# Adapter products of two tiles in one slot, one job four steps later, and the half job's second product in f16

## The reference, cut to what matters

```python
# x: (16 batches, 128 tokens, 128 features)
def moe(x, gates, shared_prob):                    # 8 experts and a shared one, F = 512
    g, u = einsum('bsd,edf->ebsf', x, Wg), einsum('bsd,edf->ebsf', x, Wu)
    experts = einsum('be,ebsd->bsd', gates, einsum('ebsf,efd->ebsd', silu(g) * u, Wd))
    shared = (silu(x @ Sg) * (x @ Su)) @ Sd
    return (1 - shared_prob) * experts + shared_prob * shared

def adapter(x, language):                          # A = 32, one of 10 languages per batch
    h = relu(einsum('bsh,bha->bsa', x, W1[language]) + b1[language])
    y = x + einsum('bsa,bah->bsh', h, W2[language]) + b2[language]
    return layernorm(y) * gamma[language] + beta[language]

x = x + moe(x, ...)
x = x + adapter(x, language)
```

## Time and profile before

| what | value |
| --- | --- |
| time, median of three runs | 297.66 us |
| time of the profiled execution | 297.04 us |
| its span | 295.2 us |
| PE busy | 290.1 us, 98% |
| DVE busy | 268.8 us, 91% |
| ACT busy | 231.1 us, 78% |
| POOL busy | 19.3 us, 7% |
| PE in the chain that ended last | 94% |

### The profile page before, as it was taken

The page is one execution under the profiler, slowest core; times in us unless marked ns, Lnnn a source line. Parts: engine busy times, 40 slices in busy tenths (PEclk is TensorE's granted clock), DMA queues, the critical chain, the costliest instruction groups (busy, mean ns, idle before and its releaser), DMA issues.

```text
span 295.2 us, 5086 instructions
## 1 busy us (share of the span) xinstructions
PE 290.1 (98%) x1510; PEld 144.3 (49%) x1510; DVE 268.8 (91%) x585; ACT 231.1 (78%) x517; POOL 19.3 (7%) x32
## 2 busy tenths in 40 slices
PE   8999999999999999999999999999999999999995
PEld 2444444444444444444444444444444444588883
DVE  5999999998989898988989999999999999977795
ACT  6998878788878787877897788887878876667771
POOL 3200201100000000000002010001100011000011
PEclk9999999999999999999999999999999999999999
DMA  6973110244000000000011001010001110000001
GB/s 208 385 307 109 52 65 19 62 120 112 2 2 0 0 2 0 0 2 1 1 22 26 18 9 39 12 25 19 17 3 39 27 18 10 2 36 3 0 2 36
DMA packets 17940, 13.39 MB, mean 45 GB/s; under 512 B 11486, under 2 KB 15994, under 8 KB 17914
## 3 DMA queue, kind: packets, MB, share of 16 engines
q1 hardware_dynamic: 17482, 12.86, 14.4%
q10 hardware_dynamic: 432, 0.21, 0.2%
HBM read 11.23 MB, written 1.05 MB: 42 GB/s over the span
## 4 chain that ended last, share of the span: by engine, by line
PE 94%; DVE 2%; DMA 1%; SPq 1%; issue 1%; ACT 0%; POOL 0%; POOLq 0%; DVEq 0%
PE moe_ps L449 10%; PE moe_ps L446 10%; PE moe_ps L447 10%; PE gate_ps L400 10%; PE up_ps L426 10%; PE up_ps L431 10%; PE up_ps L423 10%; PE gate_ps L403 10%; PE gate_ps L408 10%; DMA w_full<-weights 1%; DVE hidden L680 1%; PE adapt_ps L458 0%; DVE gx_lo L649 0%; SPq L319 0%; DVE h_lo L686 0%
## 5 line engine op out<-in xcount | busy, mean ns | idle before, releaser
L563 ACT ACTIVATE silu<-gate_ps 128x512 f32<-128x512 f32 (+1 forms) x160 | 88.2, 551 | 45.3 <-PE gate_ps L408 44.3
L680 DVE SCALAR_TENSOR_TENSOR hidden<-silu,up_ps 128x512 f32<-128x512 f32 (+1 forms) x160 | 100.3, 627 | 19.2 <-PE up_ps L431 11.6
L686 DVE TENSOR_TENSOR h_lo<-hidden,h_hi 128x512 f16<-128x512 f32 (+1 forms) x160 | 102.4, 640 | 0.2
L568 ACT ACTIVATE h_hi<-hidden 128x512 f16<-128x512 f32 (+1 forms) x160 | 92.8, 580 | 9.2 <-DVE hidden L680 8.4
L426 PE MATMUL up_ps<-gx_lo,w_hi 128*128 128x512 f16 (+1 forms) x160 | 57.3, 358 | 0.4 <-DVE gx_lo L649 0.4
L400 PE MATMUL gate_ps<-x_hi,w_hi 128*128 128x512 f16 (+1 forms) x160 | 57.4, 359 | 0.0
L431 PE MATMUL up_ps<-gx_hi,w_lo 128*128 128x512 f16 (+1 forms) x160 | 57.3, 358 | 0.0
L423 PE MATMUL up_ps<-gx_hi,w_hi 128*128 128x512 f16 (+1 forms) x160 | 57.3, 358 | 0.0
L403 PE MATMUL gate_ps<-x_lo,w_hi 128*128 128x512 f16 (+1 forms) x160 | 57.3, 358 | 0.0
L446 PE MATMUL moe_ps<-h_hi,w_hi 128*128 128x512 f16 (+1 forms) x160 | 57.3, 358 | 0.0
L449 PE MATMUL moe_ps<-h_lo,w_hi 128*128 128x512 f16 (+1 forms) x160 | 57.3, 358 | 0.0
(11 more groups left out here) (88 smaller groups left out, 148.6 us busy)
## 6 DMA issues: line engine op xcount, KB each, us to landing
w_full<-weights SPq DMA_DIRECT2D x8, 768.0 KB, 9.2
affine_sb<-affine SPq DMA_DIRECT2D x16, 128.0 KB, 2.9
x_full<-xT SPq DMA_DIRECT2D x3, 256.0 KB, 8.6
x<-x_blocks SPq DMA_DIRECT2D x48, 16.0 KB, 1.8
out_dram<-result SPq DMA_DIRECT2D x3, 256.0 KB, 2.1
w_full<-weights SPq DMA_DIRECT2D x4, 128.0 KB, 3.0
w_full<-w2b SPq DMA_DIRECT2D x24, 16.0 KB
w_full<-weights SPq DMA_DIRECT2D x1, 256.0 KB, 3.8
```

The lines of the kernel that those rows point to most:

```text
L563: nc.scalar.activation(silu_slot(n), gate_ps[n % 2][:, 0:STEPS[n][4]], ACT.Silu, scale=1.0 / W_SCALE).then_inc(silu_ready, 1)
L568: nc.scalar.activation(h_slot(h_hi, n), hidden_slot(n), ACT.Copy).then_inc(h_hi_ready, 1)
L680: nc.vector.scalar_tensor_tensor(out=hidden_slot(n), in0=silu_slot(n), scalar=HIDDEN_RESCALE, in1=up_ps[n % 2][:, 0:STEPS[n][4]], op0=ALU. ...
L686: nc.vector.tensor_tensor(h_slot(h_lo, n), hidden_slot(n), h_slot(h_hi, n), ALU.subtract).then_inc(h_lo_ready, 1)
```

## The change

Three things change. The job of tile 0 starts at step 75 instead of 71 and that of tile 1 at 95 instead of 91; `moe_out` stays where a tile's sum is ready (`moe_at`: steps 71 and 75), for which `x2T`, `w1_sb` and `b1_sb` get a second place. `adapter_in` of tiles 0 and 1 is issued together, in step 76 (`in_step`), into the two halves of each 256 columns of `adapt_ps`; tile 1's `w1` and `b1` are loaded at the start. Job 3 makes its second product as the others do: f16 parts on 98 rows, with `w2_upper` at at-8 (step 139), `w2_lower` at at-6, `h_upper` at at+4, `h_others` at at+4, two f16 matmuls at at+7 and one 256-wide `y`.

```diff
-JOBS = [(0, 0, BATCHES, down_step(0, 0) + 1), (1, 0, BATCHES, down_step(0, 0) + 21),
+JOBS = [(0, 0, BATCHES, down_step(1, 0) + 1), (1, 0, BATCHES, down_step(1, 0) + 21),
         (2, 0, BATCHES, down_step(2, 0) + 1), (TILES - 1, 0, BATCHES // 2, down_step(TILES - 1, 0) + 1)]
+def moe_at(j):
+    return down_step(JOBS[j][0], 0) + 1
+def in_step(j):
+    return JOBS[0 if j == 1 else j][3] + in_at(j)
 def back_at(j):
-    return 6
+    return 6 if j < MOVED else 7
+def w2_at(j):
+    return 0 if j < MOVED else -8
-        w1_sb = sb("w1_sb", [P, BATCHES * A], F32)
+        w1_sb = sb("w1_sb", [P, 2 * BATCHES * A], F32)
-        x2T = sb("x2T", [P, N], F32)
+        x2T = sb("x2T", [P, 2 * N], F32)
...
-            load_adapter(0)
+            load_adapter(0, True, True)
+            load_adapter(1, True, False)
...
-                    load_adapter(t + 1)
+                    load_adapter(t + 1, t > 0, True)
...
-                pe.wait_ge(adapter_loaded, adapter_count(t))
-                if j > 0:
+                pe.wait_ge(adapter_loaded, adapter_count(0 if t == 1 else t))
+                if j > 1:
                     pe.wait_ge(y_ready, BEFORE[j])
                 for q in range(first, first + count):
-                    last = nc.tensor.matmul(fourth(adapt_ps, q)[:, 0:S], cols(w1_sb, q, A), cols(x2T, q, S),
+                    last = nc.tensor.matmul(cols(fourth(adapt_ps, q), place(t), S, A), w1_of(t, q), cols(x2T_of(t), q, S),
                                             start=True, stop=True, tile_position=(0, q * A))
...
-                pe.wait_ge(adapt_h_ready, count)
-                pe.wait_ge(x2_ready, 1)
+                pe.wait_ge(w2_lower_ready, j + 1)
+                pe.wait_ge(h_others_ready, 2 * (j + 1))
+                if j >= MOVED:
+                    pe.wait_ge(x2_ready, 1)
                 for q in range(first, first + count):
-                    last = nc.tensor.matmul(cols(back_ps[q % 2], q // 2, D), stacked(adapt_h, q, S, A + 1),
-                                            stacked(w2b2_sb, q, D, A + 1), start=True, stop=True)
+                    last = nc.tensor.matmul(cols(x2_ps, q, D), cols(h_stack, q, S, STACK), cols(w2_stack, q, D, STACK),
+                                            start=True, stop=True)
...
-                if since == 2 and j < MOVED:
+                if since == w2_at(j) + 2:
                     w2_lower(j)
-                if since == 4 and j < MOVED:
+                if since == (in_at(j) + 3 if j < MOVED else in_at(j) + 2):
                     h_others(j)
```

More of the change, by code:

```diff
@@ L200, in build @@
         x2_ps = bank("x2_ps")
-        back_ps = [adapt_ps, x2_ps]
         last_tile = TILES - 1
@@ L276, in adapter_count, with place, w1_of, b1_of @@
         def adapter_count(t):
-            return 16 * BATCHES * (6 * (t + 1) if t < last_tile else 6 * t + 3)
+            return 16 * (8 * BATCHES, 12 * BATCHES, 18 * BATCHES, 18 * BATCHES + 6 * (BATCHES - TAIL[2]) + 3 * TAIL[2])[t]
+        def place(t):
+            return 1 if t == 1 else 0
+        def w1_of(t, q):
+            return cols(w1_sb, place(t) * BATCHES + q, A)
+        def b1_of(t, q):
+            return fourth(b1_sb, q)[:, place(t):place(t) + 1]
+        def x2T_of(t):
+            return cols(x2T, place(t), N)
         def fourth(tensor, q):
@@ L337, in _, with load_adapter @@
             sp.wait_ge(ids_loaded, 16)
-            def load_adapter(t):
+            def load_adapter(t, first, second):
                 for q in range(BATCHES):
@@ L342, in load_adapter @@
                     one = bass.ds(lang, 1)
-                    sp.dma_start(cols(w1_sb, q, A), w1[one].rearrange("l h a -> (l h) a")).then_inc(adapter_loaded, 16)
+                    if first:
+                        sp.dma_start(w1_of(t, q), w1[one].rearrange("l h a -> (l h) a")).then_inc(adapter_loaded, 16)
+                        sp.dma_start(b1_of(t, q), b1[one].rearrange("l a o -> (l a) o")).then_inc(adapter_loaded, 16)
                     w2b2_q = w2b2[one].rearrange("l a h -> (l a) h")
-                    if t == last_tile:
+                    if second and t == last_tile and q >= TAIL[1]:
                         sp.dma_start(stacked(w2b2_sb, q, D, A + 1), w2b2_q).then_inc(adapter_loaded, 16)
-                    else:
+                    elif second:
                         w2_q = cols(w2_full, q, D, STACK)
@@ L519, in _ @@
                 if i == 0:
-                    pe.wait_ge(adapt_h_ready, JOBS[-1][2] + 1)
+                    pe.wait_ge(adapt_h_ready, 1)
                 else:
@@ L585, in w2_upper @@
                     act.wait_ge(back_done, j)
-                nc.scalar.activation(w2_stack[:, :], w2_full[:, :], ACT.Copy, scale=W_SCALE).then_inc(w2_upper_ready, 1)
+                width = JOBS[j][2] * D
+                nc.scalar.activation(w2_stack[:, 0:width], w2_full[:, 0:width], ACT.Copy,
+                                     scale=W_SCALE).then_inc(w2_upper_ready, 1)
             def h_upper(j):
                 act.wait_ge(h_full_ready, BEFORE[j + 1])
-                nc.scalar.activation(h_stack[0:A, :], h_full[:, :], ACT.Copy, scale=H_SCALE).then_inc(h_upper_ready, 1)
+                width = JOBS[j][2] * S
+                nc.scalar.activation(h_stack[0:A, 0:width], h_full[:, 0:width], ACT.Copy,
+                                     scale=H_SCALE).then_inc(h_upper_ready, 1)
             def copy_x2(j):
@@ L626, in _ @@
                 for j, (_, _, _, at) in enumerate(JOBS):
-                    if n == at and j < MOVED:
+                    if n == at + w2_at(j):
                         w2_upper(j)
@@ L630, in _ @@
                         adapter_relu(j)
-                    if n == at + in_at(j) + 2 and j < MOVED:
+                    if n == at + in_at(j) + 2:
                         h_upper(j)
@@ L723, in norm_stats @@
                         dve.wait_ge(x2_ready, 1)
[L724 to L729 removed]
+                    width = JOBS[j][2] * D
+                    nc.vector.scalar_tensor_tensor(out=y[:, 0:width], in0=x2_ps[:, 0:width], scalar=OUT_RESCALE,
+                                                   in1=x2[:, 0:width], op0=ALU.mult,
+                                                   op1=ALU.add).then_inc(y_ready, JOBS[j][2])
                 if i == 0:
@@ L787, in _ @@
                 hidden_of(n)
-                for j, (_, _, _, at) in enumerate(JOBS):
-                    if n == at:
+                for j in range(len(JOBS)):
+                    if n == moe_at(j):
                         moe_out(j)
```

47 lines of the change are left out of this document (16 added, 31 removed).

## The result

The changed kernel takes 300.19 us (median of six runs, 299.3 to 300.55), the kernel before 297.61 us in the same comparison (297.28 to 298.52). The ratio is 1.008, with a 95% interval of 1.0065 to 1.0095: by the ratio the change costs 2.4 us, by the two medians 2.6. The prediction said 298.4 us, in 297.2 to 299.0. Its sign was right, its size of 0.7 us about a third of what was measured, and the time lies outside its range. The profiled execution took 299.3 us, with a span of 297.5 us at a granted clock of 0.998.

What follows compares the result with a forecast made beforehand. PE, busy for 98% of the span, was taken as the bound. A net +0.52 us from the moved jobs and +0.18 us from the half job gave +0.70 us on 297.66, so 298.4 us, range 297.2 to 299.0.

Steps and rivals of the forecast that it cites:

- Its sign: Whole kernel: the change makes it slower, by a sum of +0.70 us; slower was given a chance of 0.57.
- The merged slot: PE, step 76: one w1 slot of about 0.87 us replaces two, saving 0.23 us (0 to 0.44).
- The wait at 116 and 117: PE waits 0.75 us (0.6 to 0.95) for DVE's backlog at up(116) or step 117's adapter_back, as job 1 nears job 2.
- at their price: DVE beside POOL's x_beta: three such meetings stay and cost as before, where an h_lo took 0.66 us more.
- The two are one loss, not two: PE at up(116) and step 117's adapter_back: both read the same backlog, so 0.75 us is counted once.
- The 0.04 us for the signal: Step 117: of the 0.49 us to spare ahead of job 2's adapter_back, some 0.04 goes for the signal.
- Behind step 118 the backlog of the kernel before had room again, so little is added.: After step 118: DVE's backlog adds little further loss; no amount for it stands in the sum.
- job 2's weights behind job 1's moves: Rival, SP's queue: late weights make ACT's w2_upper(2) wait 0.6 us; 1 us more would give 298.9 us; chance 0.13.
- The tail: Half job, steps 151 to 154: up(154) waits for hidden(152), so the end loses 0.18 us instead of gaining 0.40.
- I take 0.75, two thirds: DVE, job 3: the two 256-wide h_others cost 0.75 us, between bounds of 0.58 and 1.17.
- The bound of -0.05: Half job at the end: the loss is -0.05 us if the h_others pair costs 0.58 us.
- the rival's sum: No-change rival (chance 0.22), one wait much smaller: sum +0.47 us, 298.1 us, if the pair in step 151 costs 0.58.

Runs made afterwards that it cites:

- experiment 4: Against the changed kernel, SP issues job 1's result store behind job 2's sixteen block moves instead of ahead of them; 298.9 us, ratio 1.0041.
- the repeated run: The changed kernel once more with no edit, for a second profile and time; 299.85 us, ratio 1.0079 to the kernel before.
- the first run: The changed kernel as first measured and profiled against the kernel before; median 300.19 us, profiled execution 299.3 us.

## Why the prediction was wrong

**The merged slot: right.** It took 0.88 us for eight products where 0.87 was forecast, and gained 0.22 against two slots, with the 0.08 us of small stalls on top.

**The wait at 116 and 117: the mechanism right, the size in half of the profiles.** Forecast were 0.75 us (0.6 to 0.95). Measured are 0.61 us in three profiles and 1.10 in three. The text left the meetings with `x_beta` "at their price", which was 0.66 us in the earlier trace rows. It is not a fixed price: at job 1's `x_beta` it was 0.48 us of `h_lo` or 1.04 us of `gx_lo`, and the earlier trace rows show one meeting only. The 0.49 us between the two kinds of profile go with these 0.56 us; no run changed that meeting alone. "The two are one loss, not two" didn't hold in the second kind, where 0.59 at 116 and 0.51 at 117 stand one behind the other; that the backlog itself was larger there would explain it. The 0.04 us for the signal was short too: from the end of the second `h_others` to `adapter_back` the changed kernel takes 236.00 - 235.85 = 0.15 us. That the 0.61 us of the first kind lie in the range is in part luck: 0.18 us less at the meeting and 0.11 us more for the signal go against each other.

**The failed step: "Behind step 118 the backlog of the kernel before had room again, so little is added."** That is true of the backlog (with the store behind the moves `up(122)` waits 0.08 us), and I looked for nothing else. What the moved job does is issue a store later, in step 113, and SP's program has that store ahead of job 2's moves, whose blocks are ready in step 112. The prediction wrote down job 2's weights behind job 1's moves as a rival, in the same queue, and stopped one entry short. That rival itself came nearly as priced (0.24 us of ACT's wait where 0.6 was forecast, none on PE):

```profile
223.33 0.63 ACT L607 ACTIVATE w_stack<-w_full 98x512 f16<-98x512 f32 x1 [0.24 <-DMA w_full<-w2b]
```

With the missed store the term behind step 118, put at nothing, was 0.26 us in one profile and 1.24 in the other, part of which is a slow issue on SP; in the medians the queue's order is worth 0.95 to 1.3 us (experiment 4).

**The tail: the mechanism right, the term mis-sized.** The step was "I take 0.75, two thirds": the pair costs 0.76 us alone, but 1.18 us here (283.24 - 282.06), since the copy of x2 that was pushed behind `h_upper` pushed POOL's `x_beta` onto it. In the kernel before it ran from 280.34 us and stretched nothing. The f16 products cost 0.11, as forecast, but PE waited 0.15 us at `gate(154)` and 0.93 at `up(154)` where the forecast had 0.6 at `up(154)` alone. With the slot's 0.52 gone that makes +0.67, and the table has +0.69, in place of +0.18. I had weighed POOL beside the whole jobs and not here, where my own edit moved it. (The bound of -0.05 given for a pair of 0.58 us was a slip: the same working gives +0.01, and the rival's sum +0.53 in place of +0.47.)

By the Trainium skill, "SBUF — State Buffer", section "Who interferes with whom", a DVE instruction with two SBUF inputs contends with a GpSimd one that reads SBUF, for a port that is locked as a whole, and issue order decides which of the two blocks. These runs agree in which instructions are stretched: `gx_lo`, `h_lo` and the second `h_others` have two SBUF inputs and end 0.15, 0.55 and 0.28 us behind `x_beta`; `hidden` with its PSUM operand isn't stretched; and where `gx_lo` wasn't, POOL took 1.49 us. They end 0.13 to 0.19 us sooner than if they had only begun when `x_beta` ended (0.34, 0.68 and 0.41 us alone). The part on issue order no run here shows, since POOL's recorded start is ahead in both kinds.

The sum, from the forecast 0.70 us: for the repeated run 0.51 more in the tail, 1.24 at step 122, 0.14 less at 116 and 117, and 0.07 less before step 94 make 2.2 us; for the first run 0.51, 0.26, 0.35 more at 116 and 117, 0.06 at step 106 and 0.07 less make 1.8 us. These are the table's sums. The first run's median of 2.6 us holds 0.7 us more than its profile's waits, and no profile shows that part in full.

## What to carry to other kernels

When a job is moved, list its last instructions as well as its first, and for each in-order queue what then stands ahead of what: a store that nobody waits for still holds up the loads behind it. When an edit moves an instruction on one engine, follow what that instruction releases on the others, POOL above all, and see what it now falls beside. A saving on PE that is paid with DVE work is a saving only in steps where DVE has that much room.

## What the runs showed of the hardware

What a DVE instruction loses beside a POOL one isn't fixed: two executions of one kernel lost 0.48 and 1.04 us at the same `x_beta`, on different instructions.

A store that stood ahead of sixteen block moves in SP's program and waited for its result kept them back for 2.20 us; with the store behind them they started 0.03 us after their data was ready. The issue of such a move takes 0.60 us in the median and up to 1.88 at the longest, so that the sixteen of job 2 took 10.3 to 11.6 us.

The start, up to step 5, varies by 1.35 us between profiles of kernels whose PE instructions are the same there. That hides effects of 0.2 us in the time of a single execution; stretches between two steps agree to 0.01 us where nothing was changed, and show them.
